# Two-layer transformer block on one core: the first feed-forward layer from two four-byte halves of x1 instead of three bf16 pieces

## The reference, cut to what matters

```python
x = layernorm(x + attention(x))          # 16 heads of 16, one shared key/value head
x = layernorm(x + ffn(x))                # the part that is changed is in here
x = layernorm(x + state_space_and_cfc(x))  # a scan over positions and a gated recurrence
x = layernorm(x + mx_quantised_linear(x))

def ffn(x):                              # x is called x1 in the kernel
    h = einsum('bsd,fd->bsf', x, ternary(W1)) + b1   # 256 -> 1024
    h = gelu(h)
    return einsum('bsf,df->bsd', h, ternary(W2)) + b2  # 1024 -> 256
```

## Time and profile before

| | |
|---|---|
| runs | 1874.81 us median, 1872.44 to 1875.64 |
| profiled execution | span 1875.9 us from the first to the last instruction; no other time of this execution is given |
| TensorE (PE) | 1757.2 us busy, 94%, 29935 matmul instructions |
| weight loads (PEld) | 1283.4 us, 68% |
| VectorE (DVE) | 1413.3 us, 75% |
| ScalarE (ACT) | 1173.6 us, 63% |
| GpSimd (POOL) | 1020.8 us, 54% |
| granted TensorE clock, mean | 0.967 of full; 0.84 up to 130 us, 1.00 from 500 to 1500 us, 0.61 after 1790 us |
| DMA | 92.94 MB |

### The profile page before, as it was taken

The page is one execution under the profiler, slowest core; times in us unless marked ns, Lnnn a source line. Parts: engine busy times, 40 slices in busy tenths (PEclk is TensorE's granted clock), DMA queues, the critical chain, the costliest instruction groups (busy, mean ns, idle before and its releaser), DMA issues.

```text
span 1875.9 us, 74519 instructions
## 1 busy us (share of the span) xinstructions
PE 1757.2 (94%) x29935; PEld 1283.4 (68%) x29935; DVE 1413.3 (75%) x2997; ACT 1173.6 (63%) x2795; POOL 1020.8 (54%) x3192
## 2 busy tenths in 40 slices
PE   6879899999999999999999999999999999999875
PEld 4545567777777777777777777777777777777653
DVE  4656767787778877787778877787778777787454
ACT  3445666666666666666666666666666666666521
POOL 2102245666566666666566666666566656666632
PEclk8889999999999999999999999999999999999965
DMA  8511111111111111111111111111111111111000
GB/s 228 162 30 37 38 45 40 42 47 48 45 43 43 51 45 45 39 50 45 45 43 46 50 45 42 42 51 45 45 41 48 48 45 45 41 48 29 20 22 21
DMA packets 140912, 92.94 MB, mean 50 GB/s; under 512 B 20196, under 2 KB 139800, under 8 KB 140568
## 3 DMA queue, kind: packets, MB, share of 16 engines
q1 hardware_dynamic: 136368, 87.91, 17.2%
q10 hardware_dynamic: 4200, 0.27, 0.2%
HBM read 31.50 MB, written 18.35 MB: 27 GB/s over the span
## 4 chain that ended last, share of the span: by engine, by line
PE 57%; DVE 19%; SPq 7%; issue 6%; DMA 4%; POOL 3%; ACT 3%; DVEq 0%; ACTq 0%; POOLq 0%
PE gen_bank L766 10%; PE gen_bank L868 9%; PE value_bank L729 8%; DVE nmax L1121 8%; PE score_bank L697 7%; PE max_banks L559 6%; SPq L414 5%; DMA lowstage<-qpiece 3%; PE gate_bank L761 2%; DVE stats L1242 2%; DVE qaug L1137 2%; PE gen_bank L581 2%; PE gen_bank L807 2%; PE gen_bank L776 2%; SPq L417 2%
## 5 line engine op out<-in xcount | busy, mean ns | idle before, releaser
L1068 ACT ACTIVATE probs<-score_bank 128x512 f32<-128x512 f32 x1024 | 604.2, 600 | 238.8 <-PE score_bank L697 226.0
L1121 DVE TENSOR_REDUCE nmax<-max_banks 128x2 f32<-128x1024 f32 x512 | 622.6, 1216 | 89.5 <-PE max_banks L561 85.5
L697 PE MATMUL score_bank<-qaug,kaug 98*128 98x512 bf16 x1024 | 370.9, 387 | 2.4 <-ACT probs L1068 1.4
L729 PE MATMUL value_bank<-probs,vaug 128*32 128x128 f32 x8192 | 332.6, 280 | 0.0
L729 PEld LDWEIGHTS value_bank<-probs,vaug 128*32 128x32 f32 x8192 | 193.9, 109 | 123.2 <-issue 93.6
L1656 POOL TENSOR_TENSOR diff<-gates 128x16 f32<-128x16 f32 x472 | 126.3, 267 | 235.1 <-ACT gates L1074 233.8
L766 PE MATMUL gen_bank<-w2T,hT 128*128 128x256 f32 x1024 | 252.1, 389 | 0.0
L559 PE MATMUL max_banks<-kaug,qaug 64*128 64x512 bf16 x512 | 199.9, 390 | 37.4 <-DVE nmax L1121 35.1
L766 PEld LDWEIGHTS gen_bank<-w2T,hT 128*128 128x128 f32 x1024 | 184.3, 190 | 33.7 <-issue 13.8
L561 PE MATMUL max_banks<-kaug,qlow 64*128 64x512 bf16 x512 | 200.8, 392 | 0.0
L868 PE MATMUL gen_bank<-x1piece,w1Tb 128*128 128x128 bf16 x3072 | 195.2, 220 | 0.5 <-DVE x1rest L1396 0.5
(11 more groups left out here) (233 smaller groups left out, 2968.2 us busy)
## 6 DMA issues: line engine op xcount, KB each, us to landing
qstage<-qpiece SPq DMA_DIRECT2D x384, 64.0 KB
lowstage<-qpiece SPq DMA_DIRECT2D x192, 64.0 KB
xt<-in_L_attn_x SPq DMA_DIRECT2D x64, 128.0 KB
xk<-in_L_attn_x SPq DMA_DIRECT2D x16, 512.0 KB, 7.4
residual<-x2s SPq DMA_DIRECT2D x64, 128.0 KB
x2f<-residual SPq DMA_DIRECT2D x64, 128.0 KB
out<-x SPq DMA_DIRECT2D x64, 128.0 KB
raw<-in_L_ffn_W SPq DMA_DIRECT2D x2, 1024.0 KB, 8.3
```

The costliest lines, as they stand in the source:

```text
L697: pe.matmul(score_bank[t % 2][:, :], kaug[0:AUG, r, tt, u, :], qaug[:, r, u, :, :].rearrange("p h s -> p (h s)"), start=True, stop=True).t ...
L729: last = pe.matmul(value_bank[32 * g:32 * g + 32, :].rearrange("p (k t) -> p k t", k=HG)[:, :, uv * BLOCK_POS:(uv + 1) * BLOCK_POS], vaug[ ...
L1068: act.activation(probs[:, t % 4, :], score_bank[t % 2][:, :], ACT.Exp).then_inc(exp_done, 1)
L1121: dve.tensor_reduce(nmax[:, m % 2, at:at + 3:2], max_banks[:, :, :], AX_X, ALU.max, negate=True).then_inc(max_taken, 1)
```

## The change

The first layer's input is kept as two halves of 12 bits in the dtype `float32r`, a four-byte format that is meant to pass TensorE once. ScalarE's copy makes the first half, VectorE's subtraction writes the second directly, and the cast and the second subtraction go, with the semaphore `x1_step`. A block is 16 products in place of 24. The weights are kept as `float32r` too, which doubles their size from 4 to 8 KB per partition. To make room, the setup's buffers are allocated in a region of their own that is closed before the later buffers (from `oT` to `xdT`) are allocated, so both lie at the same addresses. The order of every engine's work is otherwise the same.

```diff
-        w1Tb = sb("w1Tb", [P, KT, F], BF16)
+        w1T = sb("w1T", [P, KT, F], F32R)
...
+        setup_memory = ExitStack()
+
+        def setup_sb(name, shape, dt=F32):
+            return setup_memory.enter_context(nc.sbuf_tensor(name, shape, dt))
+
+        raw_q = setup_sb("raw_q", [P, KT, D])
...
+        kpiece = setup_sb("kpiece", [P, 3, S], BF16)
...
+        setup_memory.close()
         oT = sb("oT", [P, HG, P])
...
-        x1piece = sb("x1piece", [P, 3, KT, P], BF16)
-        x1rest = sb("x1rest", [P, KT, P])
+        x1half = sb("x1half", [P, 2, KT, P], F32R)
...
-                turns += [(raw_1[:, f, k * P:(k + 1) * P], P, P, w1Tb[:, k, f * P:(f + 1) * P], one, ("w1", 3))]
+                turns += [(raw_1[:, f, k * P:(k + 1) * P], P, P, w1T[:, k, f * P:(f + 1) * P], one, ("w1", 3))]
...
                             pe.wait_ge(emptied[half], use(half, name, m))
-                            for piece in range(3):
-                                if piece > 0:
-                                    pe.wait_ge(x1_step, 2 * m + piece)
+                            pe.wait_ge(emptied[0], use(0, "X1T", m) + 1)
+                            for piece in range(2):
                                 for f in range(4):
                                     for k in range(KT):
-                                        last = pe.matmul(gen_bank[half][:, f * P:(f + 1) * P], w1Tb[:, k, (4 * half + f) * P:(4 * half + f + 1) * P],
-                                                         x1piece[:, piece, k, :], start=(piece + f + k == 0), stop=(piece == 2 and k == KT - 1),
+                                        last = pe.matmul(gen_bank[half][:, f * P:(f + 1) * P], w1T[:, k, (4 * half + f) * P:(4 * half + f + 1) * P],
+                                                         x1half[:, piece, k, :], start=(piece + f + k == 0), stop=(piece == 1 and k == KT - 1),
                                                          skip_group_check=True)
...
-                            act.activation(x1piece[:, 0, :, :], g0[:, 0:D].rearrange("p (k t) -> p k t", k=KT), ACT.Copy).then_inc(x1_hi, 1)
+                            act.activation(x1half[:, 0, :, :], g0[:, 0:D].rearrange("p (k t) -> p k t", k=KT), ACT.Copy).then_inc(x1_hi, 1)
...
-                            dve.tensor_tensor(x1rest[:, :, :], g0[:, 0:D].rearrange("p (k t) -> p k t", k=KT), x1piece[:, 0, :, :],
+                            dve.tensor_tensor(x1half[:, 1, :, :], g0[:, 0:D].rearrange("p (k t) -> p k t", k=KT), x1half[:, 0, :, :],
                                               ALU.subtract).then_inc(emptied[0], 1)
-                            dve.wait_ge(emptied[0], use(0, "X1T", m) + 1)
-                            settle(dve)
-                            dve.tensor_copy(x1piece[:, 1, :, :], x1rest[:, :, :]).then_inc(x1_step, 1)
-                            dve.wait_ge(x1_step, 2 * m + 1)
-                            dve.tensor_tensor(x1piece[:, 2, :, :], x1rest[:, :, :], x1piece[:, 1, :, :], ALU.subtract).then_inc(x1_step, 1)
```

More of the change, by code:

```diff
@@ L12 @@
 BF16 = mybir.dt.bfloat16
+F32R = mybir.dt.float32r
 FP8 = mybir.dt.float8e4
@@ L183, in block_net @@
         probs = sb("probs", [P, 4, 512])
+        hT = sb("hT", [P, FT, P])
+        csum = sb("csum", [P, R, GROUP, BLOCK_POS])
+        go_on = sb("go_on", [P, GROUP, BLOCK_POS])
+        states = sb("states", [P, 2, BLOCK_POS, B])
+        hseq = sb("hseq", [P, 2, STEPS, B])
+        qscale = sb("qscale", [P, 3, D // QBLOCK])
+        square = sb("square", [P, 1])
+        stats = sb("stats", [P, 5, 6])
+        meanvar = sb("meanvar", [P, 5, 2])
+        veps = sb("veps", [P, 5])
+        rstd = sb("rstd", [P, 5])
+        LN1, LN2, LNI, LN3, LN4 = range(5)
+        setup_memory = ExitStack()
+        def setup_sb(name, shape, dt=F32):
+            return setup_memory.enter_context(nc.sbuf_tensor(name, shape, dt))
+        raw_q = setup_sb("raw_q", [P, KT, D])
+        raw_kv = setup_sb("raw_kv", [DK, 2, D])
+        raw_o = setup_sb("raw_o", [P, KT, D])
+        raw_1 = setup_sb("raw_1", [P, FT, D])
+        raw_2 = setup_sb("raw_2", [P, KT, F])
+        raw_b = setup_sb("raw_b", [P, D])
+        raw_c = setup_sb("raw_c", [P, KT, N])
+        raw_g = setup_sb("raw_g", [P, 4, D + P])
+        raw_ow = setup_sb("raw_ow", [P, KT, P])
+        raw_f = setup_sb("raw_f", [P, KT, D])
+        tern = probs[:, :, :].rearrange("p a b -> p (a b)")
+        fq = setup_sb("fq", [P, KT * D], FP8)
+        fs = setup_sb("fs", [P, 3, KT * D // QBLOCK])
+        xk = setup_sb("xk", [P, XK, TT, D])
+        xTk = setup_sb("xTk", [P, 2, KT, S])
+        kpiece = setup_sb("kpiece", [P, 3, S], BF16)
+        kvT = hT[:, FT // 2:FT, :].rearrange("p f t -> p (f t)")
+        kres = hT[:, 0:FT // 2, :].rearrange("p f t -> p (f t)")
+        setup_memory.close()
         oT = sb("oT", [P, HG, P])
@@ L190, in block_net @@
         x1b = sb("x1b", [P, D])
-        x1piece = sb("x1piece", [P, 3, KT, P], BF16)
-        x1rest = sb("x1rest", [P, KT, P])
-        hT = sb("hT", [P, FT, P])
+        x1half = sb("x1half", [P, 2, KT, P], F32R)
         x2r = sb("x2r", [P, D])
@@ L198, in block_net @@
         xnT = sb("xnT", [P, KT, P])
-        xdT = sb("xdT", [P, KT, P])
         bs = sb("bs", [P, GROUP, BLOCK_POS])
-        csum = sb("csum", [P, R, GROUP, BLOCK_POS])
-        go_on = sb("go_on", [P, GROUP, BLOCK_POS])
-        states = sb("states", [P, 2, BLOCK_POS, B])
         gates = sb("gates", [P, GW])
@@ L207, in block_net @@
         mixed = sb("mixed", [P, B])
-        hseq = sb("hseq", [P, 2, STEPS, B])
         x2f = sb("x2f", [P, D])
@@ L212, in block_net @@
         x3b = sb("x3b", [P, D])
-        qscale = sb("qscale", [P, 3, D // QBLOCK])
         qin = sb("qin", [P, D])
@@ L218, in block_net @@
         x4 = sb("x4", [P, D])
-        square = sb("square", [P, 1])
-        stats = sb("stats", [P, 5, 6])
-        meanvar = sb("meanvar", [P, 5, 2])
-        veps = sb("veps", [P, 5])
-        rstd = sb("rstd", [P, 5])
[L224 to L244, removed]
+        xdT = sb("xdT", [P, KT, P])
         k_dram = nc.dram_tensor("key_pieces", [R, TT, 2 * DK, 3 * S], BF16, kind="Internal").ap()
@@ L303, in block_net @@
         x1_hi = sem("x1_hi")
-        x1_step = sem("x1_step")
         x1b_ready = sem("x1b_ready")
```

## The result

The changed kernel takes 1942.51 us (median of 4 runs, 1938.52 to 1945.17), the kernel before 1875.22 beside it. The ratio is 1.0362, with a 95% interval of 1.0346 to 1.0378: 67 us slower. The profiled execution has a span of 1941.9 us and a time of 1943.72.

The account below looks back on a forecast made before the run. TensorE was taken to bound the kernel, nearly tied with detours over VectorE and query DMAs. +55 us on matmuls less 1 us of waits gave +54: 1930 us, 1929 against the median; own range 1918 to 1945, full range 1812 to 1945.

Parts of the forecast that it names:

- the likeliest case: Both first-layer blocks on TensorE: 2048 products at 111 ns each, +55 us, time 1929 us against the median; chance 0.48.
- the distance between starts: TensorE's dense queue in both blocks: cost is start to start, 56 ns per bf16 matmul before, 111 ns per new one.
- The load: Weight load in both blocks: 116 ns of a 128-column f32 load scale with width, not covered by a 56 ns pass.
- the stream: Moving side in both blocks: 128 four-byte columns take about 110 ns, as the transposes do.
- Rival 1: Both blocks: full-rate single pass, 56 ns per product, 57 us saved, time 1820 us; chance 0.30.
- Rival 3: Both blocks: the format is treated as plain f32, 222 ns per product, +283 us, time 2158 us; chance 0.12.
- Rival 2: Both blocks: loads partly covered, distance of 60 to 100 ns, time 1826 to 1908 us; chance 0.10.
- Every loop runs through both blocks: TensorE and the detours over VectorE and query DMAs: all pass both blocks, so the period moves by twice a block's change.
- The terms at 0: VectorE's two dropped operations (0.72 us per tile, covered), waits, ScalarE's four-byte write and shared setup memory: each costed at 0.
- the start-up: First stretch of the kernel: a few tiles may lose waits of 0.2 to 0.3 us, 1 us less.

Follow-up runs that it names:

- two-byte halves: The changed kernel with float16 in place of float32r for both x1 halves and W1: 1834.19 us, ratio 0.9788 to the kernel before.

## Why the prediction was right, and what it missed

**The direction, the place and the likeliest case held.** 1942.5 us lies in the stated range and in the forecast's own one, and the step that carried it is the distance between starts. I took 111 ns for each of the 2048; blocks A and B have 109 and 114. Between single starts it is 111 to 112. The sum was 0.86 us per tile; the two blocks measure 0.88, the commonest period 0.89 and the mean of the middle tiles 0.91.

**The load was the right reason, the stream was not.** I gave two reasons for 110 ns and trusted the stream more ("it is the moving side that takes it"), from the transposes, whose 128 columns cost 110 although one of them loads only 16. That step failed. With 64 columns moving the distance stays, with 64 loaded it falls to 63 ns. So the transposes' row did not carry over to a product's stream. What sets their own 110 ns was not tried. The row that did carry over was the f32 load: 116 ns scaled from it for 128 columns, 57 ns measured for 64.

The Trainium skill, "TensorE: Matmul & The Clock Gate", section "LDWEIGHTS (loading the stationary operand)", has a load take its columns divided by 1.2 ns, an estimate of 107 ns here, and its section on weight-path modes keeps the fast load from FP32. The runs agree and extend it to this format: 194 ns of load against 98 for both two-byte ones, and distances of 109 to 114 ns. I had let the transposes' load of 141 ns weaken it, which was the same mistake.

**Rival 1 named a true price in the wrong place.** One pass does stream at nearly full rate: 512 columns in 0.23 us, where bf16 takes 0.22. The Trainium skill, "FP8 and Floating Point Precision", section "TensorE Precision Notes", has true FP32 make four passes; the runs agree, with 0.44 us for a plain f32 product of 256 columns against 0.118 in the new format. What rival 1 missed is that "a load that no longer has to carry two parts" is still as long as before. It also took off 2 us for the gelus of block A; in the run with two-byte halves they cost 0.12 us per tile, 8 in all. **Rival 3** asked for 222 ns per product and is out; but its thought that the format is worth nothing here over plain f32 is true for the kernel as a whole, since two halves at 110 are one product at 220. **Rival 2** has its distance, 63 ns, only in the run that loads 64 columns.

**Every loop runs through both blocks: shown in both directions.** Blocks and the commonest period moved together: by +0.88 and +0.89 us in the changed kernel, and from there by -1.60 and -1.61 with half the weights. With two-byte halves TensorE stayed the limit (489.8 of 500 us busy from 1000 to 1500 us).

**The terms at 0.** VectorE's two operations and the shared memory were run alone, and both are 0 within the error. The new waits and ScalarE's write show nothing in the profile.

**What the sum lacked: 12 us.** The spans differ by 66.0 us. Of the 63 periods between block B's starts, the middle 55 are longer by 0.91 each, 50 us. The first five are longer by 10.5 in place of 4.4, the last three by 3.6 in place of 2.7, and before and behind them lies another 1.8. I had taken 1 us off for the start-up; it added 6. Two rows say what happens there. In the start-up stretch, the kernel before and then the changed one:

```profile
130.00:260.00 130.00, 118.72 (x1510) 78.24 (x1507) 87.75 (x157) 81.47 (x172) 33.62 (x93) 0.97 0.14 36
```
```profile
130.00:260.00 130.00, 117.12 (x1210) 77.60 (x1209) 74.95 (x130) 73.58 (x156) 28.27 (x76) 0.93 0.13 34
```

The granted clock is 0.93 in place of 0.97. The timeline of the changed kernel shows one of the falls:

```profile
177.76 0.58 PE L564 MATMUL max_banks<-kaug,qaug 64*128 64x512 bf16 x1 [2.33 <-DVE nmax L1125]
...
180.10 1.08 PE L734 MATMUL value_bank<-probs,vaug 128*32 128x128 f32 x16
...
182.35 0.64 PE L734 MATMUL value_bank<-probs,vaug 128*32 128x128 f32 x16
```

```profile
178.00:181.00 3.00, 3.00 (x24) 1.71 (x22) 2.33 (x6) 1.20 (x2) 1.20 (x3) 0.50 0.00 1
```

TensorE sits idle for 2.33 us, and the 16 value products behind it run at 1.08 us before they are back at 0.64: the granted clock from 178 to 181 us is 0.50, the 1.2 GHz level. The wait is for maxima that hang on the query DMAs: VectorE's copy of the queries stood idle 2.88 us for them just before (2.37 in the kernel before). There are four such waits in this stretch, 10.4 us together against 7.4 in the kernel before, where the clock also fell, but behind two of them only. The six DMA issues of a tile took 4.4 to 4.7 us in the first tiles of this run, 3.8 in those of before.

Two executions with the same short blocks show that the falls of the clock are a part of their own. First the two-byte halves, then the same with VectorE's operations put back:

```profile
146.57 0.60 PE L564 MATMUL max_banks<-kaug,qaug 64*128 64x512 bf16 x1 [2.55 <-DVE nmax L1125]
```
```profile
147.10 0.39 PE L566 MATMUL max_banks<-kaug,qaug 64*128 64x512 bf16 x1 [2.44 <-DVE nmax L1127]
```

Both have issues of 4.4 to 4.9 us and waits of 2.2 to 2.9 us. In the first the clock falls behind each of the four waits (0.91 over the stretch) and the first five periods sum to 132.4 us; in the second it stays at 1.00 behind this one (0.97 over the stretch) and they sum to 127.5. So neither the length of the blocks nor that of the issues decides alone. Each of these figures is from one execution. The shared memory is not the cause either (0.99, first five 127.1). Why the issues take longer in these kernels, and what decides whether the clock falls, was not tried and stays open.

## What to carry to other kernels

Price a matmul in a dense queue as the longer of its stream and its weight load, and look up the load by the width of its data: here 128 four-byte columns need about 110 ns, which 128 moving columns did not cover and 256 did. A format that saves passes saves stream time alone; where few columns move, fewer bytes per element do more than fewer passes, and two float16 halves gave 40 us where two float32r halves lost 67. Take the price from a row of the same kind of instruction, not of a mode that looks like it.

## What the runs showed that I had not expected

- Two-instruction f32 and two one-pass halves cost the same at 128 moving columns (1944.58 and 1942.51 us), although at 256 the plain one costs nearly four times as much.
- The clock's lower level appeared behind waits of TensorE of 2.3 us in the start-up, and one execution of a kernel with less work on TensorE (two-byte halves) was slower there than the kernel before, 132.4 against 127.5 us for five periods. Behind a wait of 2.44 us in another run the clock did not fall.
- Moving five products by one slot cost 30 us, because they had hidden a DMA that no row of the kernel's middle named.
